# The eight-head cross attention of a perceiver step: one head per 50-row half, queries read in place, maxima on 64x64 tiles

## What is computed

```python
q = LN(x) @ Wq + bq            # (32, 64, 128), 8 heads of 16
k = ctx @ Wk + bk              # (32, 1601, 128)
v = ctx @ Wv + bv
p = softmax(q_h @ k_h.T / 4)   # for each item and head: 64 x 1601
out = concat_h(p @ v_h) @ Wo + bo
```

## Time and profile before

| | us |
|---|---|
| median of 3 runs | 1934.53 (1932.29 to 1940.65) |
| the profiled execution, its own time | 1933.98 |
| its span in the profile | 1932.2 |
| first cross attention, from the start of the query transfers to the last output copy | 66.4 to 547.1 |
| second cross attention, from the first maxima | 975 to 1652 |

### The profile page before, as it was taken

One profiled execution on the slowest core, in us unless ns is written; L12 is line 12 of the kernel. 1 busy time (PEld: TensorE's weight loads), 2 busy tenths in 40 slices (PEclk: granted clock), 3 DMA queues, 4 the chain that ended last, 5 costly groups with the idle time before them and its releaser, 6 DMA issues. The chain is left out here.

```text
span 1932.2 us, 68384 instructions
## 1 busy us (share of the span) xinstructions
PE 1755.1 (91%) x29638; PEld 1107.3 (57%) x29656; DVE 1378.2 (71%) x2412; ACT 1253.0 (65%) x2205; POOL 506.0 (26%) x399
## 2 busy tenths in 40 slices
PE   7899999999989588899769999999999999847898
PEld 5577777777765365444436665666666665535443
DVE  3577777777743675566478988988988997356565
ACT  3477777777743381333348888888888888447243
POOL 4322322322130440111112222222222220033365
PEclk9799999999999677899979999999999999969899
DMA  4455555555400300456465655655655652030011
GB/s 156 104 140 152 140 143 151 138 142 152 101 4 0 67 4 17 120 147 167 107 106 105 105 95 105 103 98 105 104 98 105 103 98 28 2 68 4 28 41 42
DMA packets 66552, 178.35 MB, mean 92 GB/s; under 512 B 20276, under 2 KB 24500, under 8 KB 65844
## 3 DMA queue, kind: packets, MB, share of 16 engines
q1 hardware_dynamic: 64436, 170.85, 40.4%
q10 hardware_dynamic: 1824, 3.20, 0.7%
HBM read 84.39 MB, written 1.31 MB: 44 GB/s over the span
## 5 line engine op out<-in xcount | busy, mean ns | idle before, releaser
L648 ACT ACTIVATE Pb<-ps 128x512 f32<-128x512 f32 (+1 forms) x832 | 451.9, 597 | 49.7 <-PE ps L595 30.7
L615 PE MATMUL ps<-Pb,V 128*17 128x64 f32 (+1 forms) x13312 | 379.5, 248 | 0.7 <-ACT Pb L648 0.7
L724 DVE TENSOR_REDUCE MX<-ps 128x2 f32<-128x804 f32 (+1 forms) x385 | 363.7, 983 | 18.5 <-PE ps L561 17.3
L615 PEld LDWEIGHTS ps<-Pb,V 128*17 128x17 f32 (+1 forms) x13312 | 250.1, 97 | 86.8 <-issue 43.3
L726 DVE TENSOR_REDUCE MX<-ps 128x1 f32<-128x402 f32 (+1 forms) x512 | 265.9, 569 | 30.8 <-PE ps L565 24.9
L768 POOL TENSOR_TENSOR ABO<-CT 128x1601 bf16<-128x1601 f32 x44 | 125.8, 2862 | 536.7 <-DMA CT<-ctxT 536.7
L651 ACT ACTIVATE Pb<-ps 128x1024 f32<-128x1024 f32 (+1 forms) x224 | 204.6, 959 | 40.9 <-PE ps L599 38.2
L561 PE MATMUL ps<-KST,QW 50*128 50x402 bf16 (+1 forms) x1024 | 177.4, 342 | 13.3 <-DVE MX L724 5.6
L595 PE MATMUL ps<-QW,KST 50*128 50x128 bf16 (+1 forms) x3328 | 164.9, 218 | 5.4 <-ACT Pb L648 3.6
L671 ACT ACTIVATE V<-ps 128x512 f32<-128x512 f32 (+1 forms) x256 | 129.3, 522 | 49.4 <-PE ps L547 39.8
L565 PE MATMUL ps<-KST,QW 96*128 96x402 bf16 (+1 forms) x512 | 148.9, 340 | 6.1 <-DVE C L710 0.8
(11 more groups left out here) (248 smaller groups left out, 3071.2 us busy)
## 6 DMA issues: line engine op xcount, KB each, us to landing
CT<-ctxT SPq DMA_DIRECT2D x44, 800.5 KB, 4.8
KST<-HL SPq DMA_DIRECT2D x320, 100.1 KB, 3.0
KST<-C SPq DMA_DIRECT2D x320, 100.1 KB, 3.0
Pb<-routed SPq DMA_DIRECT2D x64, 256.0 KB, 3.9
ABO<-ctxT SPq DMA_DIRECT2D x10, 800.5 KB, 5.1
T<-ctxT SPq DMA_DIRECT2D x10, 800.5 KB, 4.5
KST<-HL SPq DMA_DIRECT2D x128, 50.0 KB, 2.7
KST<-C SPq DMA_DIRECT2D x128, 50.0 KB, 2.7
```

Source lines behind the costliest of these rows:

```text
L615: mm = nc.tensor.matmul(ps[32 * quad:32 * quad + m, SUM, oc:oc + nh * S], V[0:n, b % 2, tile, v0:v0 + m], Pb[0:n, buffer(b, x), ti * att.W ...
L648: nc.scalar.activation(Pb[0:n, buffer(b, x), i * 512:(i + 1) * 512], score_bank(b, x, i)[0:n, :], ACT.Exp, scale=att.scale).then_inc(exps, 1)
L724: nc.vector.reduce_max(MX[:, b % 2, 2 * j:2 * j + 2], work(job)[:, :, 0:n], AX.X).then_inc(freed["dve"], 1)
```

## The change

All of it concerns `XA0`, unless said otherwise.

- Stacking as in `XA1`: each head pair is cut in two, one head (16 channels) on rows 0 to 49 (32 rows high and low, 2 shift rows, 16 rows) and the other on rows 64 to 113. A stack is 16 transfers for 12 (eight of 32 rows, eight of 16 rows). For both cross attentions the transfers of groups 0 and 1 now go first by part: four of 32 rows, four of 16 rows, and then the same for groups 2 and 3.
- Queries in place: with one head per half no channel has to be zeroed, so PE reads `QS` itself; POOL's `pool_queries` falls away, and the shift rows are written into `QS` (`shift_rows`). The queries are stacked by `split_halves` (16 transfers, eight on each queue) in place of `split_rows`. PE waits for them right at the start of the "rest" part, ahead of the values of item 0.
- Maxima: 8 jobs for 16. A job has four matmuls with 50 rows and 64 columns of queries on the four 64x64 tiles of the array (two heads of two groups), and fills two banks; DVE reduces both in one instruction (two, where the pair of banks is the last and the first).
- Scores: for each tile of keys 8 matmuls of 50 rows by 128 keys with 64 columns moving, for 4 of 98 rows with 128 columns. The even heads go to one bank and the odd ones to the other, and ACT has one exponential of 512 columns per bank (256 in the last unit), two for one. Three banks for scores, four for K, V, M and R.
- R0: the same four matmuls, now on two row pairs; ACT copies one pair of rows, DVE the other (256 columns each).
- A new `ORDERS[8]`.
- The rows of ones in `KST` and the zeroed rows of `QS` are set once at the start; a memset of 16.1 us on POOL between this attention and the self attention goes.

The heart of the diff:

```diff
-    8: ("K0 K1 P-1 H0 K2 H1 H2 K3 V0 H3 S0 M0 M1 V1 M2 M3 S1 S2 M4 M5 M6 P0 P1 M7 M8 S3 M9 S4 M10 P2 M11 M12 V2 M13 "
-        "S5 M14 S6 M15 V3 P3 P4 P5 R0 ")}
+    8: ("M0 K0 K1 S0 H0 P-1 H1 M1 K2 K3 S1 H2 H3 V0 M2 P0 S2 M3 M4 P1 S3 V1 V2 M5 S4 P2 M6 M7 S5 P3 P4 V3 S6 P5 R0 ")}
...
-        self.mjobs = [(u, c0, n) for u in range(4) for c0, n in self.kchunks]
+        self.mjobs = [(u, c0, n) for u in range(2 if self.single else 4) for c0, n in self.kchunks]
...
-            self.score_banks, self.sum_bank, self.work_banks = (3, 3, 4) if self.halved else (4, 4, 3)
-            self.stacks = 8 if self.halved else 6
+            self.score_banks, self.sum_bank, self.work_banks = 3, 3, 4
+            self.stacks = 8
...
             def pe_maxima(b, j):
...
+                for h in range(2):
+                    if att.single:
+                        for i in range(2):
+                            g = 2 * u + i
+                            mm = nc.tensor.matmul(work(job)[64 * i:64 * i + 64, h, 0:n], queries(b, h, g),
+                                                  KST[half[h], b % 3, g, c0:c0 + n], start=True, stop=True,
+                                                  skip_group_check=True, tile_position=(64 * h, 64 * i))
...
-                else:
-                    mm = nc.tensor.matmul(work(job)[:, 0:n], QW[0:RAW, b % 3, g * 128:(g + 1) * 128],
-                                          KST[0:RAW, b % 3, g, c0:c0 + n], start=True, stop=True)
...
             def pe_scores(b, x):
...
+                        for h in range(2):
+                            if att.single:
+                                col, wide, moving = ti * 256 + g * S, S, queries(b, h, g)
...
+                            mm = nc.tensor.matmul(score_bank(b, x, h)[0:n, col:col + wide],
+                                                  KST[half[h], b % 3, g, k0:k0 + n], moving,
+                                                  start=True, stop=True, tile_position=(64 * h, 0))
...
             def act_exp(b, x):
...
+                wide = len(att.exps[x]) * att.W // 2
...
-                    nc.scalar.activation(Pb[0:n, buffer(b, x), 0:banks * 512].rearrange("p (a c) -> p a c", a=banks),
-                                         score_banks(b, x)[0:n, 0:banks, :], ACT.Exp, scale=att.scale).then_inc(exps, 1)
+                for i in range(2):
+                    nc.scalar.activation(Pb[0:n, buffer(b, x), i * 512:i * 512 + wide], score_bank(b, x, i)[0:n, 0:wide],
+                                         ACT.Exp, scale=att.scale).then_inc(exps, 1)
...
             def sp_stack(b):
...
+                for p in range(2):
+                    landed = s_kst[b % 3][p]
+                    for part in range(2):
+                        for g in (2 * p, 2 * p + 1):
+                            for h in range(2):
+                                a, c0 = 64 * h, 32 * g + 16 * h
+                                rows, taken = (KST[a:a + 32], slice(0, 2)) if part == 0 else (KST[a + 34:a + 50], 0)
+                                eng.dma_start(rows[:, b % 3, g, :], keys(b)[c0:c0 + 16, taken, 0:NK]).then_inc(landed, 16)
...
             if role == "pe":
-                eng.wait_ge(sem("ones_set"), 2 + past)
+                eng.wait_ge(sem("ones_set"), 4)
+                if att.single:
+                    eng.wait_ge(*inputs_ready)
                 eng.wait_ge(ready, past + 1)
                 pe_value_bias()
```

More of the change, by code:

```diff
@@ L44 @@
 SLOTS = 4
+TWO_ONES = float(np.array([0x3F803F80], np.uint32).view(np.float32)[0])
 ORDERS = {
@@ L86, in __init__ @@
         self.units = heads // 2
-        self.halved = heads == 16
-        self.parts = 2 if self.halved else 1
+        self.single = cross and heads == 8
         q4 = 402
@@ L101, in columns, with probabilities @@
     def columns(self, head):
-        return (head // 2 % 2 * 8 + head // 4 * 2 + head % 2) * S if self.halved else head * S
+        return (head // 2 % 2 * 8 + head // 4 * 2 + head % 2) * S
+    def probabilities(self, head, ti):
+        return head % 2 * 512 + ti * 256 + head // 2 * S if self.single else self.columns(head)
     def products(self):
@@ L508, in score_bank @@
                 return ps[:, (2 * unit(b, x) + i) % att.score_banks, :]
-            def score_banks(b, x):
-                first, last = sorted((2 * unit(b, x) + i) % att.score_banks for i in range(2))
-                return ps[:, first:last + 1:last - first, :]
             def scored(b, x, parts):
-                return exps, units + att.parts * unit(b, x) + parts
+                return exps, 2 * (units + unit(b, x)) + parts
             def buffer(b, x):
@@ L573, in pe_shift_rows @@
                 banks_free(job)
-                for g in range(4):
-                    for h in range(2) if att.halved else (None,):
-                        unit_at, row = (g, 96) if h is None else (2 * g + h, 32 + 64 * h)
-                        mm = nc.tensor.matmul(work(job)[row:row + 2, g * 128:(g + 1) * 128], MH[:, b % 2, unit_at, :],
+                for u in range(att.units // 2):
+                    for h in range(2):
+                        row = 32 + 64 * h
+                        mm = nc.tensor.matmul(work(job)[row:row + 2, u * 128:(u + 1) * 128], MH[:, b % 2, 2 * u + h, :],
                                               wb("ident16"), start=True, stop=True, tile_position=(0, row))
@@ L700, in act_shift_rows @@
                 eng.wait_ge(*filled_with(job))
-                row = 32 if att.halved else 96
-                nc.scalar.activation(QW[row:row + 2, b % 3, :], work(job)[row:row + 2, :], ACT.Copy).then_inc(freed["act"], 1)
+                nc.scalar.activation(shift_rows(b, 0), found_rows(job, 0), ACT.Copy).then_inc(freed["act"], 1)
             def dve_keys_low(b, j):
@@ L896, in cross_attention @@
                     for kind, j in att.order:
-                        if kind == "M" and j == 0 and b + 2 < B:
+                        if kind == "M" and j == 0 and b + 2 < B and not att.single:
                             pool_queries(b + 2)
```

139 lines of the change are left out of this document (54 added, 85 removed).

## The result

The changed kernel takes 1946.48 us (median of 13 runs, 1938.93 to 1954.79) where the kernel before takes 1932.29 beside it (13 runs, 1926.55 to 1942.62): the ratio is 1.0068, interval 1.0051 to 1.0086. It is slower by 13 to 14 us where I had forecast 13 us less, and it lies outside the range of 1903 to 1944. The profiled execution took 1953.73 us, its span is 1951.7; so the trace lies 7 us above the median.

What follows compares the result with a forecast made beforehand. PE was taken as the bound, 13.9 of 14.51 us in a loop body (95%). The profiled 1933.98 us, less 24.3 in the loop, plus 11.5 at the start, gave 1921.2, rounded to 1921; range 1903 to 1944.

Steps and rivals of the forecast that it cites:

- The new body: First cross attention's loop: waits between engines set the body's length, 13.7 us for 14.51, saving 24.3 us over 30 full bodies.
- The walk: One body followed along the new order, 0.1 us between engines: R0 returns after 13.6 us, wrapped banks add 0.1.
- rivals 2 and 4: Score matmuls at 0.025 us: 1939, chance 0.22; weight loads bound small matmuls or tiles run singly: 1963, chance 0.05.
- The changes of tiling: On PE, each change of the array's tiling loses 0.095 us; 24 for 8 in a body, +1.5 us.
- Rival 1: Loop body as short as its work: ACT's 12.2 us at 95% gives 12.9 us, kernel 1897; chance 0.12.
- Rival 3: M0 waits for its stacked keys: 14.55 us from M0 to M0, kernel +13 us, 1947; chance 0.11.
- the sign that I had named for this: In the loop, M0 waiting for `KST`, released by a DMA, would show the prediction wrong.
- 5.4 + 7 x 0.75 + 2.8: Time from M0 until stacked keys land: last low part and issue, seven more issues, landing; forecast 13.2 us, cost nothing.
- The start: Before the loop, PE waits first for the stacked queries, starting at 79.2 us; fewer maxima give back 0.5: +11.5 us.
- Tail 0, POOL 0: Last two bodies: gains and the cost of scores on three banks cancel, 0; POOL's dropped work changes nothing.

Runs made afterwards that it cites:

- wide_tiny: Changed kernel with context loads cut to 16 rows of 64 bytes and 52 score matmuls of 128 columns for 104 of 64 (output wrong): ratio to before 0.9912.
- after_tiny_context: Changed kernel with the first cross attention's context loads cut to 16 rows of 64 bytes from item 3 on (output wrong): ratio to before 0.9975.
- the control: Kernel before with the first cross attention's context loads cut to 16 rows of 64 bytes from item 3 on (output wrong): ratio 0.9993.
- before_split_four: Kernel before with each score matmul of 128 columns written as four of 32: ratio to before 1.0442.
- spread_one: Changed kernel with PE's query wait moved to the first maxima, GpSimd behind the first shift, and two product units for one in the next body: ratio 1.0050.

## Why the prediction was wrong

The step that failed is "**The new body** ... 13.7 us for 14.51, 0.8 us in each of 30 full bodies: -24.3". The walk itself was right: without stalls a body takes 13.56 us in the changed kernel and 13.47 in wide_tiny. What failed is that the walk took it for granted that PE always has its next instruction. I had counted 52 more score matmuls and 16 more for the maxima as columns and as changes of tiling, not as instructions: with a weight load each they are 136 more in a body (809 in a full body for 672). 28.0 us of stalls for 2.7 turn -28 (31 bodies by 0.9) into -2.7. That the stalls cost the kernel this time, and are not idle time that something else would have filled, is shown by after_tiny_context and wide_tiny (18 and 30 us less than the changed kernel, by the ratios) beside the control's nothing.

Point by point:

- **PE.** The four maxima tiles run at once (two jobs of 402 columns, eight matmuls, in 0.54 us where two of the old matmuls took 0.51), and a score unit of sixteen starts within 0.41 - 0.19 = 0.22 us, 0.014 each. So my rivals 2 and 4 are both refuted, and the floor of 25 ns that the Trainium skill gives (TensorE: Matmul & The Clock Gate, "Back-to-back issue gap") doesn't hold for 64 columns on two halves. It does show for 32 columns on the whole array, 0.024 us in before_split_four. The changes of tiling cost what I had charged: sixteen scores that start within 0.22 us are followed by the first product 0.34 us after their first start (281.62 to 281.96).

```profile
122.54 0.54 PE L556 MATMUL ps<-KST,QS 50*64 50x402 bf16 x8
...
158.46 0.41 PE L591 MATMUL ps<-QS,KST 50*128 50x64 bf16 x16
```

- **ACT.** I said 12.2 us in a body; 159.17 us in 203 are 11.3 for a body of 14.46. Two exponentials of one bank take 1.08 us, where one of two banks took 0.97 in the mean of two: +0.11 and not +0.17, and the copies shrank. DVE was right: 155.81 in 203 is 11.1 for 11.2.
- **Rival 1** (12.9 us) is refuted by wide_tiny: 13.47 without its stalls.
- **Rival 3** named the right side and the wrong wait. M0 waits for its keys three times, 2.5 us in the whole loop (100 to 540), so the sign that I had named for this did show, at a tenth of the stalls' size. SP sends sixteen in 12.04 us, 0.75 each, which was the rival's condition, not the 0.69 I took:

```profile
PE ps L556 <- DMA KST<-C: 2.5, 3, 1.2
...
115.32 12.04 SPq L782 DMA_DIRECT2D KST<-C  x16
```

  Landing takes 2.8 us, though, not 3.9, and 5.4 + 7 x 0.75 + 2.8 = 13.45 just fits. What the fuller DMA engines delayed was the instructions, which stood in no term.
- **The start** was +8.0 for +11.5. The queries take 12.4 us and not 12.8, the keys of item 1 took 1.9 us less because the clock was up (2.1 us at 1.00 for 4.0 at 0.50), a thing that I had not priced, and maxima and shift ran 1 us faster; direction and mechanism held.
- **"Tail 0, POOL 0"** missed two terms of some 3 us each that no part of the diff touches: the clock in the tail and the collision of POOL and DVE.
- The change of sign, then: -24.3 + 11.5 = -12.8 forecast; -2.7 + 8.0 + 3.3 + 3.5 = +12.1 in the trace without the late fall of the clock, +13 in the medians.

What stays open: why the stalls of before_split_four are short, what sets the 1.2 us by which a packet starts after its block even without the context's loads, why the clock falls in the tail and behind some long stalls and not behind others, and whether a context load in smaller pieces, early enough, would help.

## What to carry to other kernels

When a change puts more and smaller instructions on a full engine, count them, also over the densest stretch: here 256 PE instructions in under some 3.7 us outrun their own supply, whatever the array could do. A transfer for which nobody waits can still cost time by standing ahead of the instructions on the DMA engines. "Issue" idle in the middle of a unit whose operands are all there is the sign: lay windows from stop to stop and add the counts. Look at the granted clock behind such stops too, before you put a longer body down to the order of the work.

## What the runs showed of the hardware

- PE's instructions come in blocks of 256, one 16 KB packet each, each requested while the block ahead of it runs: 1.0 us for the packet (0.9 to 1.9), 1.3 to 1.8 until PE goes on, and up to 3.9 us of delay at a DMA share of 0.66. Late starts up to 2.0 us (2.7 in spread_one).
- The granted clock sometimes fell to 1.2 GHz for 3 to 7 us behind stalls of 1.2 to 2.6 us: 19 of the 21 falls in the loops of twelve traces stand there. Such a microsecond costs some 0.3 to 0.45 us.
- A 128x8 operation of DVE takes 2.87 us in place of 0.17 if a 128x1601 operation of POOL starts 0.01 us ahead of it; 0.2 us decided it.
- Sixteen stacking transfers hold SP for 12.1 us in the median in the first cross attention (DMA share 0.66) and 11.3 in the second (0.47).
